# Two decoder layers on one core: zeros written by transfers, and a second part's zero fills as block scatters by GpSimd

## The reference

```python
x = x + _L0_xattn_ref(ctx, ctx, _layernorm(x), ...)
x = x + _L0_ffn_ref(_layernorm(x), gate_w, w1, w3, w2, e_bias)   # 32 experts, 4 per token
x = x + _L1_xattn_ref(_layernorm(x), ctx, ctx, ...)
x = x + _L1_ffn_ref(_layernorm(x), gate_W, W_gate, W_up, W_down)
```

## Time and profile before

| | us |
|---|---|
| median of 3 runs (840.79 to 849.19) | 841.55 |
| profiled execution | 845.37 |
| its span, first to last instruction | 843.6 |
| PE busy, share of the span | 618.1, 73% |
| DVE busy | 573.9, 68% |
| ACT busy | 439.1, 52% |
| POOL busy | 408.8, 48% |
| granted clock of PE, mean | 0.876 |

### The profile page before, as it was taken

The page is one execution under the profiler, slowest core; times in us unless marked ns, Lnnn a source line. Parts: engine busy times, 40 slices in busy tenths (PEclk is TensorE's granted clock), DMA queues, the critical chain, the costliest instruction groups (busy, mean ns, idle before and its releaser), DMA issues.

```text
span 843.6 us, 14399 instructions
## 1 busy us (share of the span) xinstructions
PE 618.1 (73%) x4127; PEld 413.5 (49%) x4155; DVE 573.9 (68%) x1570; ACT 439.1 (52%) x954; POOL 408.8 (48%) x437
## 2 busy tenths in 40 slices
PE   3598798778878676978995787688742114999991
PEld 1243344334334475867993433354321113888880
DVE  2767879879899886758874757868556665444443
ACT  2296787785878666747642343445420011555542
POOL 3316537376768572511656276767300003666741
PEclk9998999888999898989995899989965555999996
DMA  6497998655779342554766010100030000111115
GB/s 167 167 302 241 307 313 302 192 185 199 239 234 317 121 135 84 152 150 136 198 164 237 17 34 20 43 2 14 1 125 1 0 0 22 42 47 47 48 33 160
DMA packets 97478, 109.61 MB, mean 130 GB/s; under 512 B 12597, under 2 KB 81018, under 8 KB 97018
## 3 DMA queue, kind: packets, MB, share of 16 engines
q1 hardware_dynamic: 70138, 85.20, 31.4%
q0 software_dynamic: 6592, 13.51, 5.6%
q10 hardware_dynamic: 20672, 9.97, 4.1%
HBM read 84.19 MB, written 24.44 MB: 129 GB/s over the span
## 4 chain that ended last, share of the span: by engine, by line
PE 37%; DVE 32%; ACT 8%; issue 8%; SPq 6%; DMA 5%; POOL 3%; DVEq 1%; ACTq 0%; POOLq 0%
PE PS L2313 4%; PE PS L2096 4%; DVE NMp L1613 3%; PE PS L2289 3%; PE PS L2294 3%; DMA oh<-index 3%; PE PS L2109 2%; DVE oh L1462 2%; PE PS L2304 2%; PE PS L2218 2%; SPq L482 2%; PE PS L2191 2%; PE PS L2189 2%; PE PS L2241 1%; PE PS L2027 1%
## 5 line engine op out<-in xcount | busy, mean ns | idle before, releaser
L695 POOL DMA_INDIRECT yb<-ys,yrow x64 | 62.0, 969 | 79.0 <-DVE Kbd L1532 30.8
L786 POOL DMA_INDIRECT xg<-xrows,tok x39 | 37.5, 961 | 102.8 <-DVE tok L1811 91.3
L647 POOL DMA_INDIRECT xs<-xn,row x64 | 68.0, 1062 | 39.1 <-DVE row L1328 21.3
L1462 DVE TENSOR_SCALAR oh<-oh,pcol 128x2048 bf16<-128x2048 bf16 x80 | 67.9, 849 | 18.1 <-DMA oh<-index 17.0
L2022 PE MATMUL PS<-oh,T 128*128 128x512 bf16 x212 | 63.5, 404 | 17.5 <-ACT oh L926 15.4
L2027 PE MATMUL PS<-oh,T 128*32 128x512 bf16 x960 | 70.9, 404 | 0.5 <-issue 0.4
L2096 PE MATMUL PS<-xT,wgu 128*96 128x128 f32 x512 | 71.3, 286 | 0.0
L925 ACT ACTIVATE oh<-oh,pcol 128x512 bf16<-128x512 bf16 x80 | 57.8, 722 | 14.4 <-DMA oh<-index 14.4
L2096 PEld LDWEIGHTS PS<-xT,wgu 128*96 128x96 f32 x512 | 64.1, 173 | 0.0
L2036 PE MATMUL PS<-ident,gs 128*128 128x128 f32 x320 | 53.4, 290 | 11.9 <-ACT vv L947 11.5
L926 ACT ACTIVATE oh<-oh,pcol 128x512 bf16<-128x512 bf16 x80 | 57.8, 722 | 2.6
(11 more groups left out here) (410 smaller groups left out, 1618.5 us busy)
## 6 DMA issues: line engine op xcount, KB each, us to landing
oh<-index SPq DMA_DIRECT2D x80, 512.0 KB, 4.0
oh<-index SPq DMA_DIRECT2D x80, 128.0 KB, 5.3
x<-xs SPq DMA_DIRECT2D x128, 64.0 KB
ys<-y ACTq DMA_DIRECT2D x64, 128.0 KB
xs<-nil SPq DMA_DIRECT2D x56, 64.0 KB
w<-in_w SPq DMA_DIRECT2D x8, 384.0 KB, 5.7
xs<-nil SPq DMA_DIRECT2D x7, 320.0 KB
wg1r<-in_wg SPq DMA_DIRECT2D x1, 2048.0 KB, 8.1
```

Of the source, the lines that this page charges most:

```text
L647: pool.indirect_dma_start(xs[:], bass.IndirectOffsetOnAxis(ap=row0[:, QT * b + t, k:k + 1], axis=0), xn1[:, b % 2, t, :], None).then_inc(s ...
L695: pool.indirect_dma_start(yb[:, b % 2, t, k, :], None, ys[b // 2][:], bass.IndirectOffsetOnAxis(ap=yrow0[:, QT * b + t, k:k + 1], axis=0))\
L1462: dve.tensor_scalar(main, main, pcol[:, 0:1], None, ALU.is_equal).then_inc(s["oh_main"], 1)
```

## The change

Three things are changed. The zeros of `NMp`, `V2d` and `V1` are written by three transfers that SP issues, with `nil` repeated as the source, behind the loads of the first six pairs. The 32 fills of part 1 become four block scatters by GpSimd, between the eighth and the ninth row scatter of the last batch: each takes one offset for each of the 128 partitions and writes there 4 KB, eight rows, out of `NMp`, which is still zero then; one scatter serves eight experts. And DVE makes the offsets for them: from the ends of all experts it picks with a mask the one that each partition needs (partition p serves expert p/16 of its eight) and adds eight times p mod 16. The table of constants `pcol` gets two columns for it. Semaphore counts follow: who waited for the memsets waits for `fill_out`, and the number of `tables_made` is one less.

```diff
+FILL_ROWS = 8
+FILLS = E0 * P // FILL_ROWS // P
@@ SP
+            sp.wait_ge(s["g_ps"], ALL_STEPS)
+            for z in (NMp[:].rearrange("p g t c -> p (g t) c"), V2d[:].rearrange("p b g c -> p (b g) c"), V1[:].rearrange("p b (g c) -> p (b g) c", c=D)):
+                sp.dma_start(z, nil[:].unsqueeze(1).to_broadcast([P, z.shape[1], D])).then_inc(s["fill_out"], 16)
             for m in range(XPAIRS, PAIRS):
-                if 0 <= m - XPAIRS - SP_FILLS_PAIR < SP_FILLS // 3:
-                    fill_ends(1, 3 * (m - XPAIRS - SP_FILLS_PAIR), 3, "last_fill_out")
                 if m == PART_PAIRS:
-                    sp.wait_ge(s["tables_made"], 4)
-                    sp.wait_ge(s["last_fill_out"], 16 * E0)
+                    sp.wait_ge(s["tables_made"], 3)
+                    sp.wait_ge(s["last_fill_out"], 16 * FILLS)
@@ POOL
-            for z in (V2d[:], NMp[:], V1[:]):
-                pool.memset(z, 0.0).then_inc(s["zeros_made"], 1)
...
             for n in range(QT * K0):
+                if n == QT * K0 // 2:
+                    pool.wait_ge(s["rows_made"], B + 2)
+                    pool.wait_ge(s["fill_out"], 16 * (E0 + EXPERT_LOADS + 3))
+                    for i in range(FILLS):
+                        pool.indirect_dma_start(xs[:], bass.IndirectOffsetOnAxis(ap=foffi[:, i:i + 1], axis=0),
+                                                NMp[:].rearrange("p g t c -> p (g t c)"), None).then_inc(s["last_fill_out"], 16)
                 scatter_rows(B - 1, n)
@@ ACT
-            def fill_ends(n):
-                first = SP_FILLS + n * FILLS_AT_ONCE
-                _, rows = nc.values_load_multi_w_load_instructions(efilli[0:1, 1, first:first + FILLS_AT_ONCE], [mybir.EngineType.Activation],
...
-                for row in rows:
-                    act.dma_start(xs[bass.ds(row, P)], nil[:]).then_inc(s["last_fill_out"], 16)
...
-                act.wait_ge(s["zeros_made"], 3)
+                act.wait_ge(s["fill_out"], 16 * (E0 + EXPERT_LOADS + 3))
@@ DVE
-                    dve.tensor_copy(efilli[:, 1], efill[0:1, 1]).then_inc(s["tables_made"], 1)
+                    c.link(dve.scalar_tensor_tensor(out=fsel[:], in0=irow[:, 0:E0 // FILLS].unsqueeze(1).to_broadcast([P, FILLS, E0 // FILLS]),
+                                                    scalar=pcol[:, 10 + GH:11 + GH], in1=efill[:, 1].rearrange("p (n e) -> p n e", n=FILLS),
+                                                    op0=ALU.is_equal, op1=ALU.mult))
+                    c.link(dve.reduce_sum(foff[:], fsel[:], AX_X))
+                    c.link(dve.tensor_scalar(foff[:], foff[:], pcol[:, 11 + GH:12 + GH], None, ALU.add))
+                    dve.tensor_copy(foffi[:], foff[:]).then_inc(s["rows_made"], 1)
@@ PE
-                    pe.wait_ge(s["tables_made"], 4)
+                    pe.wait_ge(s["tables_made"], 3)
```

More of the change, by code:

```diff
@@ L233, in seq_kernel @@
         efill = sb("efill", [P, PARTS, E0])
-        efilli = sb("efilli", [1, PARTS, E0], I32)
+        efilli = sb("efilli", [1, E0], I32)
+        fsel = sb("fsel", [P, FILLS, E0 // FILLS])
+        foff = sb("foff", [P, FILLS])
+        foffi = sb("foffi", [P, FILLS], I32)
         nil = sb("nil", [P, D])
@@ L472, in load_experts, with fill_ends @@
                 sp.dma_start(spare[:, rows], nil[:].unsqueeze(1).to_broadcast([P, rows.stop - rows.start, D])).then_inc(s["fill_out"], 16)
-            def fill_ends(part, first, n, filled):
-                if part == 0 and first == 0:
+            def fill_ends(first, n):
+                if first == 0:
                     sp.wait_ge(s["tables_made"], 1)
-                if part == 1 and first == 0:
-                    sp.wait_ge(s["tables_made"], 3)
-                _, rows = nc.values_load_multi_w_load_instructions(efilli[0:1, part, first:first + n], [mybir.EngineType.SP], min_val=0, max_val=XS_ROWS - P,
+                _, rows = nc.values_load_multi_w_load_instructions(efilli[0:1, first:first + n], [mybir.EngineType.SP], min_val=0, max_val=XS_ROWS - P,
                                                                    skip_runtime_bounds_check_because=TABLE_IN_RANGE)
                 for row in rows:
-                    sp.dma_start(xs[bass.ds(row, P)], nil[:]).then_inc(s[filled], 16)
+                    sp.dma_start(xs[bass.ds(row, P)], nil[:]).then_inc(s["fill_out"], 16)
             def store_index(b):
@@ L507, in _ @@
                 if g >= FIRST_FILLS_STEP:
-                    fill_ends(0, 2 * (g - FIRST_FILLS_STEP), 2, "fill_out")
+                    fill_ends(2 * (g - FIRST_FILLS_STEP), 2)
             for n in range(ALL_STEPS - FIRST_FILLS_STEP, E0 // 2):
-                fill_ends(0, 2 * n, 2, "fill_out")
+                fill_ends(2 * n, 2)
             def rows_from(i):
@@ L973, in tail_values @@
                 act.wait_ge(s["v_ps"], B + b + 1)
-                act.wait_ge(s["zeros_made"], 1)
+                act.wait_ge(s["fill_out"], 16 * (E0 + EXPERT_LOADS + 3))
                 for j in range(GH):
@@ L1013, in _ @@
                     values(m - VALUES_PAIR)
[L1014 to L1017, removed]
                 if 0 <= m - BANDS_PAIR < 4 * B:
@@ L1466, in experts_of @@
                 if i == 0:
-                    dve.wait_ge(s["tables_made"], 2 * part + 2)
+                    dve.wait_ge(s["tables_made"], part + 2)
                 _, n = nc.values_load_multi_w_load_instructions(tabi[part][0:1, 1, i:i + 4], [mybir.EngineType.DVE], min_val=0, max_val=E0 - 1,
@@ L1550, in add_result @@
                     if t == 0:
-                        dve.wait_ge(s["zeros_made"], 2)
+                        dve.wait_ge(s["fill_out"], 16 * (E0 + EXPERT_LOADS + 3))
                     dve.wait_ge(s["gathered%d" % t], 16 * K0)
@@ L2076, in experts_of @@
                 if i == 0:
-                    pe.wait_ge(s["tables_made"], 2 * part + 2)
+                    pe.wait_ge(s["tables_made"], part + 2)
                 _, e = nc.values_load_multi_w_load_instructions(tabi[part][0:1, 1, i:i + 4], [mybir.EngineType.PE], min_val=0, max_val=E0 - 1,
@@ L2332, in _layout @@
     slot = (p % 32) // HD
-    pc = np.zeros((P, 10 + GH), f)
+    pc = np.zeros((P, 12 + GH), f)
     pc[:, 0] = p
@@ L2343, in _layout @@
     pc[:, 9 + GH] = -1
+    pc[:, 10 + GH] = p // (P // FILL_ROWS)
+    pc[:, 11 + GH] = p % (P // FILL_ROWS) * FILL_ROWS
     a["pcol"] = pc
```

10 lines of the change are left out of this document (3 added, 7 removed).

## The result

The changed kernel takes 831.92 us, the median of 12 runs (826.96 to 839.22), against 842.86 for the kernel before in its 12 (840.79 to 850.38). The ratio is 0.9849, with a 95% interval of 0.9817 to 0.9882: 12.7 us faster, between 9.9 and 15.4. The two medians by themselves lie 10.9 apart. The forecast had 13.8 of gain and 827.7 us. The profiled execution took 829.93, its span is 828.1 (843.6 before), the mean granted clock 0.872.

What follows compares the result with a forecast made beforehand. It blamed three places in the first layer's expert stage: memsets blocking copies, ACT's fill issues, SP's fill issues. 6.3 + 2.1 + 6.4 − 0.5 − 0.5 = 13.8 us off the 841.55 median gave 827.7 us, range 822 to 838.

Steps and rivals of the forecast that it cites:

- A: Turns 10 to 12 (starts of TensorE's transposes per pair): GpSimd's memsets block DVE weight copies; removing them gains 6.3 us.
- Both signs: Near 316 us: no DVE copy above 1.6 us, and a granted clock of 0.9 or more behind it.
- E: Zeros by SP's transfers, landing between 301 and 306 us: 0.5 us of stall as turn 6 waits for its load.
- B: Turns 20 to 25: ACT issues two fills every second pair; dropping these stops gains 2.1 us.
- C: Turns 25 to 31: SP's fill issues and register loads make TensorE wait for loads; dropping them gains 6.4 us.
- rival 4: Turns 25 to 31: the transfers themselves were the bound, so 6.4 us is lost, 834 us; chance 0.08.
- D: Four block scatters amid GpSimd's row scatters: 1.27 us each, SP waits for all before loading pair 32; cost 0.
- the cover: Spare time at turn 32: scatters allow it at 367.9 us, the work reaches it at 368.2, so 0.3 us.
- Offsets: On VectorE, one small cast becomes four linked small instructions, some 0.2 us each: 0.5 us lost.
- Rival 3: ACT's result stores stall beside the blocks' 4 KB pieces, 1 to 2 us a pair: 830 to 836 us; chance 0.12.
- Rivals 1, 2 and 4: The second of these: zeros land late, turn 6 waits 3 to 5 us, clock falls: 831 to 835 us; chance 0.12.
- rival 1: Block scatters cost by rows moved, 8.0 us each, so turn 32 is late: 11.8 us slower, 854 us; chance 0.10.

Runs made afterwards that it cites:

- blocks_only: Changed kernel with GpSimd's memsets back and no zero transfers, block scatters kept: 833.91 us, ratio 0.9880 to the kernel before.
- zeros_only: Kernel before with the three zero transfers in place of GpSimd's memsets, nothing else of the change: 840.25 us against 845.29, ratio 0.9937.
- issues_back: Changed kernel with SP's 24 issues and 8 register loads back, each writing 16 rows instead of 128 to an unread scratch tensor: 841.49 us, ratio 0.9967.
- changed_again: The changed kernel once more, unedited, beside two later runs: 832.48 us, ratio 0.9868 to the kernel before.
- blocks_early: Changed kernel with the four block scatters after four row scatters instead of eight: 832.73 us, ratio 0.9888 to the kernel before.
- memsets_between: Changed kernel without zero transfers; GpSimd writes the zeros by ten memsets of 512 columns, each behind a row scatter of batch 2: 831.15 us, ratio 0.9874.
- zeros_spread: Changed kernel with the zeros in ten transfers of 256 KB, one ahead of the loads of each of pairs 6 to 15: 829.07 us, ratio 0.9858.
- eight_blocks: Changed kernel with eight block scatters of four rows instead of four of eight rows, the same bytes: 837.2 us, ratio 0.9932.
- offsets_later: Changed kernel with VectorE's offset work taken out of loop 16 into three instructions in loops 17, 18 and 19: 832.64 us, ratio 0.9847.

## Why the prediction was right

**A, memsets: right, 6.85 against 6.3.** The 0.7 that I took off for the copies and the small memset left on GpSimd was not needed. Both signs came: a copy group of 0.43, a clock of 1.00. blocks_only, with the copy back at 5.17, and zeros_only show the cause.

**E, zeros by transfer: 1.40 against 0.5, and at another place.** I charged 0.5 for turn 6 waiting for its load. Turn 6 waits for nothing. What was charged instead is 1.4 us in the first turns, nearly all between turn 2 and turn 3 (5.48 for 4.12): VectorE stands 1.02 ahead of the copies at 297.24, while the DMA share is 0.97. The chain in order of time names what it stands for, the load of an expert number into a register, here after and then before:

```profile
296.22 0.88 DVEq L1467
...
296.01 0.12 DVEq L1468
```

With the zeros in flight this load takes 0.78 in zeros_only, 0.90 in issues_back, 0.76 in changed_again and 0.71 in blocks_early; in blocks_only, memsets_between and the two kernels with spread zeros, without three large transfers in flight, it takes 0.12. zeros_only shows the loss (26.26), blocks_only lacks it (25.22), and zeros_spread takes most of it away. Why the register load is longer beside the transfers stays open. The clock is also lower there, 0.69 and 0.74 for twelve us in which it was 0.94 and 1.00 before; but blocks_only has 0.78 and 0.93 in these stretches and loses nothing, so the clock isn't shown to be the cost. Also mis-sized were SP's three issues, 1.5 us by my sum and 4.35 by the rows; this cost nothing, since there were six pairs in hand.

**B: right, 2.07 against 2.1.** No issue idle of 1 us stands ahead of ACT's copies there. With SP's issues back and ACT's away (issues_back) the column keeps its gain but for the wait at turn 25; with both at their places (zeros_only) it is 12.61 as before.

**C: right in its mechanism, 7.73 against 6.4.** The mis-sized term is the pace of turns 25 to 31 without a wait. I took that of the six pairs behind, 2.5 us a pair; it was 2.29 (13.72/6). "Steady period" was too strong: the groups of fills come 3.38 to 4.45 us apart, every second one with a table load between, and what speaks for the sequencer is that it waits for no other engine between them. issues_back settles the dispute with rival 4 and with the rule of the Trainium skill, DMA: Bandwidth & Descriptors, "Issuing engines are not separate DMA queues": with an eighth of the bytes the old time returns, so here the sequencer's time was not small beside the transfers; it was the bound.

**D, block scatters: the price was right, the cover was gone.** 1.26 from start to start, as I had taken it over 8.0, and eight_blocks confirms that it is paid per instruction. But turn 32 alone waits, 0.93 us, the sign that I had named for it; column 31–32 costs 1.09. Three terms of my timing were off. The first scatter began at 337.90 instead of 336.6, pushed by E. Four of the last six were longer by 2.86 us together. And from the last scatter's end to turn 32 it is 4.34 (365.81, 370.15), where I had charged 6.2. With the scatters at their usual length, the last would end at 362.95 and turn 32 could start at 367.3, before the 369.06 of the work (367.47 + 1.59): there would be 1.8 us of cover. So the omission is the step that the scatters' 1.268 held to the end, taken from the earlier trace rows, while the change had moved them beside VectorE's key bands. My own alarm, a last scatter after about 362, went off by 4.1 us, and only 1.1 was lost: 1.9 were taken up by the term behind it (4.34 for 6.2), 0.9 by the work, which was itself later than I had it (369.06 for 368.2), and 0.3 by the cover. That is luck, not foresight.

**Offsets: 0.97 against 0.5** (turn 19 to 20, 3.04 for 2.07). The four together last 1.18 us, from 340.21 to 341.39, on the path; offsets_later moves them off it.

**Rival 3 came in part.** ACT waits for its stores 1.33 and 1.32 us at 358.33 and 360.78, and turn 27 to 28 takes 3.09 where its neighbours take 1.9 and 2.45. The DMA share of 350 to 356 is 1.05, and the chain in order of time has 5.17 us of "DMA ys<-y" from 355.54. In blocks_early, with the blocks' transfers earlier, the wait comes earlier too (1.20 at 350.70), and these waits are 1.6 us in all from 284 to 445 us, instead of 3.0; in eight_blocks, with half as much behind each offset, they are 1.3. I put it at about 1 us of C, by the turn; C came in larger regardless.

**Rivals 1, 2 and 4 did not come**: the blocks are not slow, turn 6 waits for nothing, and the bytes of the transfers were not the bound. In rival 1 the gain left at 2.5 us a block should have read 9.2, not 10: four times 1.23 is lost, less the cover of 0.3.

By its own terms: 6.85 + 2.07 + 7.73 + 0.39 − 1.40 − 1.09 − 1.09 − 0.22 = 13.24 at turn 37, against a sum of 13.8. A, B and C together were 1.9 larger than forecast, and the losses 2.8 larger (with 0.4 of gain behind turn 32 that I had put at nothing): that the sum is off by 0.6 only is in part luck. The terms that failed in it are E, D and the offsets, 1.0 by forecast and 3.6 in the trace. The time of 827.7 came out 4.2 too low: 1.3 of it is the base (841.55 from 3 runs, 842.86 from 12), the rest the smaller distance of the medians.

## What to carry to other kernels

Lay the stage against one event that occurs once per pair and read the intervals: three odd intervals, each with one engine behind it, gave nearly the whole sum. A sequencer is a resource like an engine: three transfers with addresses in registers cost it 1.4 us and their register loads 0.7 to 1.0 more, with 64 KB each or with 8, and here one indirect transfer of 128 offsets did the work of eight of them in 1.26. When a change moves an instruction, price it beside its new neighbours, and look at what the next wait will take back: here an edit worth 0.9 us at its place lost it again at turn 32, and neither it nor the one worth 0.7 could be told in the time.

## What the runs showed of the hardware that I had not expected

- Twenty memsets of 0.26 us in a row on GpSimd kept a VectorE copy out for 5.85 us, about as long as three large ones did (5.15). With a scatter between each two, the copies took 0.82 to 1.34 instead of 0.43.
- An indirect scatter of 128 offsets takes GpSimd 0.96 us with 512 bytes, 2 KB or 4 KB behind each offset.
- Such scatters stretch to 1.5 to 2.1 us beside VectorE instructions with both inputs in SBUF, by about the length of these: 43 of 44 long ones in thirteen traces. The weight copies of 0.43 run beside many scatters of 0.96.
- One and the same register load of VectorE's, between turns 2 and 3, took 0.71 to 0.90 us in five traces with three large transfers in flight, and 0.12 in five without them.
- Of three transfers of 1 MB or half of it, each a repeated source in pieces of 512 bytes, the first two kept SP's sequencer 0.68 and 0.66 us, the third 3.01. Ten of 256 KB, one for each pair, took 0.60 to 0.68 each.
